# Eight of 440 row gathers per sum pass moved from GpSimd's gather queue to single-row copies issued by SyncE

## The reference

```python
# layer 0
agg = segment_sum((x @ M)[src], dst, 3125);  out = relu(x @ W + agg)
# layer 1: two graph attention layers with 4 heads; layer 2: three attention blocks with 8 heads and an MLP
# layer 3
msg = h[src] * edge_weight[:, None]
agg = segment_sum(msg, edge_type_8 * N + dst, 8 * N).reshape(8, N, 8, 32)
out = einsum('rnbi,rbio->nbo', agg, weight).reshape(N, 256)
```

## Time and profile before

| what | value |
|---|---|
| median of three executions | 7132.12 us (7111.1 to 7143.51) |
| the profiled execution, its time | 7125.7 us |
| its span | 7124.0 us |
| busy in the span: PE, DVE, ACT, POOL | 4450.9, 3946.7, 3581.0, 3726.1 us |
| first pass, POOL's gathers | start 821.1 to 1476.3 us |
| second pass, POOL's gathers | start 6449.9 to 7078.3 us |
| q0 (POOL's gathers), q1 (SP's transfers) | 30.5% and 10.5% of the 16 DMA engines' span |

### The profile page before, as it was taken

One profiled execution on the slowest core, in us unless ns is written; L12 is line 12 of the kernel. 1 busy time (PEld: TensorE's weight loads), 2 busy tenths in 40 slices (PEclk: granted clock), 3 DMA queues, 4 the chain that ended last, 5 costly groups with the idle time before them and its releaser, 6 DMA issues. The chain is left out here.

```text
span 7124.0 us, 82903 instructions
## 1 busy us (share of the span) xinstructions
PE 4450.9 (62%) x21728; PEld 3312.9 (47%) x21728; DVE 3946.7 (55%) x9715; ACT 3581.0 (50%) x9073; POOL 3726.1 (52%) x3967
## 2 busy tenths in 40 slices
PE   4544354545667366755667895677795667795444
PEld 3443233323444233444555694555694545683332
DVE  7222222245667366675878545778544877673223
ACT  3333132234444344455656575666575666565554
POOL 0666566646662666425666225666234666225664
PEclk6555566666667676787888897888897888896666
DMA  1111233333441344336666226666325666433332
GB/s 59 52 50 46 65 98 93 93 93 106 113 113 59 112 113 111 88 114 201 195 196 192 87 83 186 195 194 194 98 80 176 194 197 191 125 107 114 93 91 87
DMA packets 395664, 864.27 MB, mean 121 GB/s; under 512 B 93353, under 2 KB 203851, under 8 KB 391763
## 3 DMA queue, kind: packets, MB, share of 16 engines
q0 software_dynamic: 209680, 608.73, 30.5%
q1 hardware_dynamic: 177296, 246.02, 10.5%
q10 hardware_dynamic: 8243, 4.30, 0.2%
HBM read 743.33 MB, written 115.44 MB: 121 GB/s over the span
## 5 line engine op out<-in xcount | busy, mean ns | idle before, releaser
L769 POOL DMA_INDIRECT ring<-tab_kv,idx_i x1044 | 988.4, 947 | 644.4 <-issue 291.0
L769 POOL DMA_INDIRECT ring<-tab_z,src_i x880 | 835.6, 950 | 501.5 <-issue 251.2
L845 PE MATMUL pp<-ring,scratch 128*128 128x264 f32 x1760 | 786.1, 580 | 424.7 <-DVE acc L1043 227.1
L1218 PE MATMUL pp<-ring,oh 128*128 128x256 f32 x1760 | 603.9, 496 | 641.7 <-issue 301.5
L788 PE MATMUL pq<-Qs,oht 128*128 x4176 | 679.5, 310 | 467.2 <-DVE X L955 245.6
L1043 DVE TENSOR_TENSOR acc<-acc,pp 128x264 f32 x1576 | 668.9, 424 | 377.9 <-PE pp L845 98.9
L1352 DVE TENSOR_TENSOR acc<-acc,pp 128x256 f32 x880 | 370.4, 421 | 890.1 <-DMA tab_z<-zs 272.0
L875 ACT ACTIVATE oht<-oht,part_c 128x1024 bf16<-128x1024 bf16 x284 | 325.2, 1145 | 1008.3 <-DMA oht<-lo_row_p 563.2
L1218 PEld LDWEIGHTS pp<-ring,oh 128*128 128x128 f32 x1760 | 408.3, 248 | 837.7 <-issue 730.1
L788 PEld LDWEIGHTS pq<-Qs,oht 128*128 128x128 bf16 x4176 | 436.5, 109 | 687.6 <-issue 560.7
L845 PE MATMUL pp<-ring,X 128*128 128x264 f32 x2088 | 653.5, 443 | 148.9 <-DVE acc L1043 55.1
(11 more groups left out here) (361 smaller groups left out, 9110.8 us busy)
## 6 DMA issues: line engine op xcount, KB each, us to landing
oht<-lo_row_p SPq DMA_DIRECT2D x174, 256.0 KB
oht<-lo_row_s SPq DMA_DIRECT2D x110, 256.0 KB
drow<-in_dst SPq DMA_DIRECT2D x25, 1024.0 KB
tab_h<-hs SPq DMA_DIRECT2D x25, 1024.0 KB, 4.4
tab_kv<-X SPq DMA_DIRECT2D x50, 396.0 KB, 2.7
tab_kv<-X SPq DMA_DIRECT2D x50, 384.0 KB, 3.4
ring<-tab_kv,idx_i POOLq DMA_INDIRECT x1044
ring<-tab_z,src_i POOLq DMA_INDIRECT x880
```

Source lines behind the costliest of these rows:

```text
L769: nc.gpsimd.indirect_dma_start(out=one(w, c, 0, row), out_offset=None, in_=table, in_offset=bass.IndirectOffsetOnAxis(ap=idx[:, w * WC + c ...
L845: last = nc.tensor.matmul(pp[(w * NU + n) % NB][:, 0:W8], oh[:, w % 2, UC * n + c, :], one(w, UC * n + c, 0, W8), start=(c == 0), stop=(c ...
L1218: last = nc.tensor.matmul(bank[:, c * D:(c + 1) * D], oh[:, b, 2 * k + c, :], ring[:, b, k, c, :], start=True, stop=True)
```

## The change

POOL's loop ends after 216 pairs, so the last eight chunks of each pass are not gathered. SP fetches their rows instead, one DMA per row: for each of the eight chunks and each group of 16 rows it loads 16 row numbers from SBUF into registers (L1092 of the kernel after), and then issues 16 DMAs of one row of 256 floats each (L1097), from the table in HBM at the address of the register to one partition of the first eight tiles of H. That is 1024 DMAs and 64 register loads per pass. Each chunk has a semaphore of its own, which reaches 16 * 128 when its rows are all there; PE waits for two of them per pair in the last body, in place of the gathers' semaphore, and reads the rows from H. The row numbers must lie in one partition's row for the register load, so in the first pass DVE copies two fields of the sorted records, `row_src` and `row_i8`, before their transposition. In the first pass SP's fetching stands behind its last store (keep_link), in the second it stands at the start of the pass.

```diff
@@ sum_edges
+        by_row = row_src if sort else row_i8
         with stage() as s:
+            own = H[:, 0:BODY, :]
+            s_ri = s.sem("ri")
+            s_row = [s.sem(f"row{c}") for c in range(BODY)]
+            def single_rows(e):
+                for c in range(BODY):
+                    for r0 in range(0, P, 16):
+                        _, at = nc.values_load_multi_w_load_instructions(
+                            by_row[LASTC + c:LASTC + c + 1, r0:r0 + 16], engines=[mybir.EngineType.SP], min_val=0,
...
+                        for r in range(16):
+                            e.dma_start(own[r0 + r:r0 + r + 1, c, :], table[bass.ds(at[r], 1), :]).then_inc(s_row[c], 16)
@@ sync
                         e.dma_start(keep_link, link_p[:, :, :].rearrange("p w e -> p (w e)")).then_inc(s_r, 16)
+                        e.wait_ge(s_ri, 2)
+                        e.wait_ge(s_h, 1)
+                        single_rows(e)
                         e.wait_ge(s_r, 160)
+                else:
+                    @blk.sync
+                    def _(e):
+                        single_rows(e)
@@ gpsimd
-                    for p in range(CHS // 2):
+                    for p in range((CHS - BODY) // 2):
@@ tensor
-                            e.wait_ge(s_g[b][k], i * 32 + 32)
+                            if u < NBODY - 1:
+                                e.wait_ge(s_g[b][k], i * 32 + 32)
+                            else:
+                                e.wait_ge(s_row[2 * k], 16 * P)
+                                e.wait_ge(s_row[2 * k + 1], 16 * P)
@@ vector
                         nc.vector.tensor_copy(idx[:, :], pp[0][:, 0:CHS]).then_inc(s_src, 1)
+                        for to, f in ((row_src, F_SRC), (row_i8, F_I8)):
+                            nc.vector.tensor_copy(to[0:LNS[-1], :], field(rt, LG - 1, LNS[-1], f)).then_inc(s_ri, 1)
```

More of the change, by code:

```diff
@@ L133, in build @@
     masks = keep("masks", [P, T, NT])
+    row_src = keep("row_src", [P, P], I32)
+    row_i8 = keep("row_i8", [P, P], I32)
+    LASTC = LNS[-1] - BODY
     @contextmanager
@@ L1078, in sum_edges @@
     def sum_edges(idx, table, lo_s, tile_, w_s=None, sort=None):
+        by_row = row_src if sort else row_i8
         with stage() as s:
+            own = H[:, 0:BODY, :]
[6 more added lines that the diff above has]
+                            by_row[LASTC + c:LASTC + c + 1, r0:r0 + 16], engines=[mybir.EngineType.SP], min_val=0,
+                            max_val=table.shape[0] - 1,
+                            skip_runtime_bounds_check_because="they are row numbers of the table")
+                        for r in range(16):
+                            e.dma_start(own[r0 + r:r0 + r + 1, c, :], table[bass.ds(at[r], 1), :]).then_inc(s_row[c], 16)
             ring = s.sb("ring", [P, RB, BP, 2, D])
@@ L1218, in step @@
                                 last = nc.tensor.matmul(bank[:, c * D:(c + 1) * D], oh[:, b, 2 * k + c, :],
-                                                        ring[:, b, k, c, :], start=True, stop=True)
+                                                        ring[:, b, k, c, :] if u < NBODY - 1 else own[:, 2 * k + c, :],
+                                                        start=True, stop=True)
                             last.then_inc(s_p, 1)
```

## The result

The changed kernel takes 7844.06 us in the median of 4 runs (7832.38 to 7852.77), the kernel before 7128.56 (7111.1 to 7143.51). The ratio is 1.100, with a 95% interval of 1.0985 to 1.1015: about 715 us slower. The forecast was 7122, in a range of 7090 to 7340. It missed in size and in sign: the case it held likeliest, fetching that lies hidden, did not happen. The rival "SP is late" did, for another reason than the one it gave.

What follows compares the result with a forecast made beforehand. POOL's gathers, themselves held by stalls, were taken to pace each sum pass. 7125.7 - 10.4 (POOL) + 0.4 (DVE copies), SP's fetching hidden, gave 7115.7; with the median 6.4 above, 7122 us, range 7090 to 7340.

Steps and rivals of the forecast that it cites:

- fetching that lies hidden: Main case for both sum passes: SP's fetching hidden under POOL's gathers, some 10 us gained; chance 0.46.
- SP is late: Rival: SP's 1024 register-addressed DMAs outlast POOL's gathers and PE waits; e.g. +133 us; chance 0.31, plus 0.05 within 36 us.
- The saving on POOL: POOL, each pass: eight gathers fewer save 10.0 us, less 4.8 for pairs still summed: 5.2, bounds 0 and 15.
- The price of a row by itself: SP: 0.32 + 0.05 + 0.10 = 0.47 us per row, 74 us of register loads, 555 us per pass.
- The rule that I weighed against it: Trainium skill's 512 sequencer cycles per DMA instruction on SP, 0.427 us and more, making a row some 0.57 us.
- The fetching is covered by POOL's 432 gathers, and costs nothing.: SP, both passes: fetching done 39 us ahead of the first pass's end and 84 us ahead of the second's.
- the 5 us allowed: From SP's last issue to the pass's end: 2.7 us for landing, the rest for a pair on PE and DVE.
- its threshold of 0.508 us per row: SP's row price above which the first pass's cover is gone, at T = 594 us; second pass 0.551.
- Its far end: Rival's far bound on SP: 1.51 + 0.14 = 1.65 us per row, T = 1764, about 9410 us.
- The unexplained wait: DVE, first pass: 54 remote waits, 256.7 us together, ascribed to the PE, DVE and POOL hand-over, not the gathers' data.
- SP's stream disturbs the hand-overs: Rival: a thousand more DMAs and semaphore writes lengthen DVE's waits, +51 us less 10, 7173 us; chance 0.06.
- Data on one DMA engine: SP's rows probably all go to one DMA engine, at 0.045 us a row, costed at nothing.

Runs made afterwards that it cites:

- the paced kernel: The changed kernel with a memset of 128 x 330 behind each POOL gather, so a gather every 1.51 us: 7084.55 us, ratio 1.0033.
- the one with few gathers: The changed kernel with only the first 32 gathers of each sum pass issued, their data reused by all later products: 6889.28 us.
- with plain DMAs: The changed kernel with SP's row addresses fixed in the DMAs, without register operations, moves or register loads: 7186.83 us, beside 7063.94 for the kernel before.
- with mostly two instructions per row: The changed kernel with SP's rows written out straight, the first chunk's row numbers serving all eight chunks, and one semaphore: 7474.57 us.
- with a short queue of gathers: The changed kernel with POOL waiting, before each pair of gathers, until the pair two before it has landed: 7757.1 us.
- in a loop: The changed kernel with SP's rows fetched in loops of eight turns, the first chunk's row numbers serving all chunks, and one semaphore: 8293.19 us.

## Why the prediction was wrong

- **The saving on POOL.** 10.0 us of gathers per pass, of which I let 5.2 count, 10.4 in all. Without SP's rows the kernel gained 13 to 26 us. My bounds of 0 and 15 per pass hold it; the whole 10.0 per pass would have been the better value. In the changed kernel POOL's first to last start shrank by 7 and 4 us, and nothing came of it.
- **The price of a row by itself.** I had 0.47 us, from 0.32 of L415, 0.05 for the register address and 0.10 for the register operation, and 74 us of loads, T = 555 us. Undisturbed, in the tail, 758 rows take 377 us; taking off the 47 loads that they contain at 1.254 and 0.04 us, 0.42 us each, and with 64 x 1.29 = 83 us of loads T is some 510 us. Where POOL fetches little, the rows ran from 893.3 to 1402.2, 509 us. So this term, which I called the weakest, was too high by a tenth. The rule that I weighed against it, 0.427 us for the DMA instruction alone, is not borne out: 0.225 us here. A register load of 16 values, which I had from PE at 1.107 us, takes 1.254 us on SP.
- **"The fetching is covered by POOL's 432 gathers, and costs nothing."** This is the step that failed. I priced SP's instructions from stretches in which no gathers run (L414, L1645) or where another engine had them at their middle value, and then laid them under 580 us of gathers. There each costs 0.76 us in the mean, so that a row took 2.2 us and not 0.47: 266 rows were done instead of all 1024, and the other 758 came after POOL's end.
- **The rival "SP is late".** Its sum held: the last issue plus the 5 us allowed gives 1858.5 and 7805.4 for the ends of the passes, and they came at 1858.0 and 7804.9; PE waited for `s_row` in the last body, in both passes. No run lies near its threshold of 0.508 us per row. Its cause was wrong: a DMA with an address from a register takes 0.225 us, and one with a fixed address 0.253. That its direction came true, at 0.31, is therefore luck and not foresight. Its far end, 1.51 us per issue, was meant as a queue's backlog and came from L1643; no run here shows what made it.
- **The unexplained wait.** I wrote of the 54 remote waits that I could not name the cause and that it belonged to the hand-over between PE, DVE and POOL. They go when these gathers come every 1.51 us (1.9 us left), so they hang on the gathers' pace, and I was wrong to set them apart from the gathers. They are more than slow instructions on DVE: with a gather every 1.34 us all of DVE's 308 register operations between 900 and 1350 us take 57 ns, and 158.7 us of such waits remain. There DVE and POOL go on together, 2.4 us after the modelled end of PE's product: at 1208.70 and 1208.69 us, in one such wait, behind a product whose end stands at 1206.28. What is late between these engines stays open. For SP's price the trace of before had a sign all the same, a register operation on DVE with a middle value of 57 ns and a maximum of 730. I used the 57 and left the 730.
- **SP's stream disturbs the hand-overs.** Not by much: DVE's waits that no engine ends were 256.7 us, 54 times, in the first pass, and are 234.0 us, 34 times, under another name; the stretch of gathers is 2 and 3 us shorter than it was, where eight gathers fewer could have made it 10.
- **Data on one DMA engine** at no cost: right, as far as the paced kernel and the one with few gathers show it, where rows run at full pace. Whether all rows went to one DMA engine is not shown.
- **Slips in the working.** At T = 641 us the two passes add up to some 39 us and not 36; 0.49 + 0.10 is 0.59 and not 0.60 us per row; and 0.427 + 0.05 + 0.10 is 0.58 and not 0.57. Nothing hangs on them.

## What to carry to other kernels

An instruction's price is to be read where it will run: look in the trace for the same engine, or any engine, beside the same neighbour, and at the maximum as well as at the middle value. A wait that no record explains is a price of unknown size for whatever is put there next; settle it before work is laid under it. And where many small instructions must run beside back-to-back gathers, count instructions, not their durations, and see whether a slightly slower pace of the gathers is cheaper than the slowing.

## What the runs showed of the hardware

While POOL's indirect gathers of 128 rows start every 1.25 us, an instruction of SP costs about 0.75 us in the mean over 450 us (0.76 in the changed kernel, 0.81 with plain DMAs, 0.77 with mostly two instructions per row, 0.65 with a short queue of gathers, 0.87 in a loop), whether it is a register move of 29 ns or a DMA of 225. At 1.34 us it is hardly better (260 rows in 450 us beside 194), at 1.51 nearly gone (820), at 1.73 and 2.68 gone (903). It does not go by bytes, nor by POOL's share. DVE has such long register operations too (up to 1.39 us in the changed kernel's first pass), but fewer: in the slow spell of SP that begins at 1202.8 us, DVE adds at its usual pace up to 1213. ACT has no register or semaphore instruction of 0.6 us or more in the whole trace of the kernel before or of the changed one.

The slow spells of SP follow POOL's pauses. In the changed kernel POOL stops ten times for more than 4 us between 900 and 1350 us; SP is at full pace again 3.4 to 6.4 us after the last gather's end, and slow again 1.3 to 3.5 us after POOL goes on (gathers end at 1031.05 and go on at 1036.79, SP is quick from 1035.9 to 1039.7). That would fit a backlog that must drain. What it is stays open; no experiment here reached it, and the kernels tried were all of gathers with 128 pieces.

One chip was different. The gathers of another stage, in the kernel at a pace of 1.51 us on that chip (its pause is in the sum passes only), then in the kernel before on the chip of the first profile:

```profile
L772 POOL DMA_INDIRECT ring<-tab_z,src_i x880: 942/946/1143, 1447.2 to 2646.0; - x176
```

```profile
L769 POOL DMA_INDIRECT ring<-tab_z,src_i x880: 940/946/1156, 1547.7 to 2988.0; - x176
```

The gathers are as long, but 880 of them take 1199 us there and 1440 here. It fits a chip on which 1.25 us per gather is not too fast, and then the pause's 0.26 us x 864 = 225 us less the 13 to 26 us of the eight gathers, should be lost, where 199 were. What the changed kernel does on such a chip was not measured. Nor was it tried whether a slower pace pays in that other stage, which the 240 us suggest.
